# A graph network's first stage: the table of the nodes left out, edge lists turned on TensorE, and gathers that wait for TensorE's tiles

## The chip, the cores and the metric

One core of one Trainium2 chip runs the kernel. The metric is the device time of one execution in microseconds; the times given are medians of several runs. TensorE (PE in the profile) multiplies and transposes, VectorE (DVE) and ScalarE (ACT) do the arithmetic on tiles, GpSimd (POOL) issues the indirect gathers and scatters, SyncE (SP) issues the plain DMAs.

## What is computed

Four graph layers over 10,000 nodes of 768 values and 12,500 edges (2,500 drawn edges and one loop at each node), each followed by a residual and a layer norm. Only the first of them touches the change:

```python
def gat_conv(x, src, dst, W, a_src, a_dst, bias, H, C, n):
    h = (x @ W).reshape(n, H, C)
    s_src = (h * a_src).sum(-1)
    s_dst = (h * a_dst).sum(-1)
    e = leaky_relu(s_src[src] + s_dst[dst], 0.2)
    emax = segment_max(e, dst, num_segments=n)
    ee = exp(e - emax[dst])
    denom = segment_sum(ee, dst, num_segments=n)
    alpha = ee / denom[dst]
    out = segment_sum(alpha[:, :, None] * h[src], dst, num_segments=n)
    return out.reshape(n, H * C) + bias

# first layer
out1 = gat_conv(x_norm, src, dst, W1, a_src1, a_dst1, b1, 4, 192, N)
out2 = gat_conv(out1, src, dst, W2, a_src2, a_dst2, b2, 2, 96, N)
return concatenate([x, out2], axis=-1) @ Wu + bu

# later layers, per edge
norm = dinv[src] * dinv[dst]      # dinv = 1 / sqrt(degree)
```

## The kernel before

All of the change lies in the first stage, `first_layers`. It sends 2 x 79 tiles of 128 nodes through TensorE. Tiles 0 to 78 are the normalised x times the folded weights `w1` (792 columns: h1 and the scores of both attentions, worked into the weights); tiles 79 to 157 are x times `wu`. A tile is six transposes (`turn_over`, L1123) and 36 matmuls with split operands (`multiply`, L1139). DVE takes the statistics, makes the low part (`low`, L666) and empties the product (`end`, L674 to L679); ACT normalises and makes the high part; SP loads x four tiles ahead and stores the results four tiles behind (`load`, `store`).

Beside the tiles runs the graph work. Each engine's program is written as a row of such pieces, and `bg.to(t)` runs the engine's own tile steps up to step t before the next piece. So a piece has a fixed place between two tiles on each engine, and a wait in it holds up the engine's tiles behind it. The constants `AT_...` set these places. In order:

- POOL places the edges that aren't loops as records (source, destination) in DRAM, `packed`: 25 turns of four indirect scatters (`place`, L458 to L463).
- PE counts the nodes' degrees with one-hot matmuls (L1154). DVE makes from them the number of own loops and 1/sqrt(degree) of each node; SP writes both as the table `nodes`, 79 x 128 rows of two floats (`AT_NODE`, L412).
- SP reads the records back: column-wise, one edge a partition and chunk of 128 (`sd_c`, L415), and row-wise, one chunk a partition (`sd_r`, L416), with each chunk's neighbours. DVE makes the index lists `src_i`, `dst_i` from `sd_c` and the marks of equal destinations from `sd_r`, in blocks at steps 30 to 34 (`AT_LISTS`, L724 to L770).
- POOL gathers `nodes` at both ends of the edges: 20 chunks, each of two indirect gathers of 128 rows (L479 to L484). DVE takes from it `edge_dinv` and `own_e` at step 68 (`AT_OWN`).
- First attention: POOL waits for all stores of tiles 0 to 78, clears its buffers, gathers the scores `sc1` (two gathers a chunk, 40 in all, L512 to L514), and DVE, PE and ACT weigh them at steps 90 to 97 (`AT_A`). Then come 20 chunks, one a tile: POOL gathers the rows of h1 into a ring of four, DVE folds them, PE adds them up, ACT copies, POOL puts them into `h2` (`put`, L542).
- Second attention: POOL clears `kept_rows`, gathers the rows of `h2` (40 gathers again, L580 to L582), and from step 127 (`AT_B`) they are weighed and, two chunks a tile, added up and put into `out2`.

With 2,500 edges drawn, 20 chunks hold all of them; the loops for more chunks (`rest_groups`) don't run. The stage ends when all engines are through; the next one then starts with a clearing on POOL.

## Time and profile before

| | us |
|---|---|
| median of 3 runs | 4335.33 (4334.88 to 4337.32) |
| profiled execution | 4339.43 |
| its span | 4337.6 |
| PE busy | 3720.0 (86%) |
| DVE busy | 2597.3 (60%) |
| ACT busy | 1178.5 (27%) |
| POOL busy | 625.8 (14%) |
| first stage, to PE's last matmul | about 1445 |

The busy time is a mean over stages with different limits. The windows view gives it by stretches; the granted clock (PEclk) is TensorE's, 1.00 being 2.4 GHz. In a timeline each row is one instruction or a few alike, with the idle time of its engine ahead of it and what ended it. "issue" stands for idle time in which the engine waited for nothing that the profile shows. Tile numbers in the text count the groups of six transposes of L1123 from 0.

### The profile page before, as it was taken

To read this page: it belongs to the slowest core of one execution; us is meant where nothing else is said; L and a number is where in the kernel's file an instruction comes from. 1 tells how busy PE (TensorE), PEld (TensorE's weight loads), DVE (VectorE), ACT (ScalarE), POOL (GpSimd) and SP (SyncE) were. 2 spreads that over 40 slices of the span, in tenths; PEclk is the share of its full clock that TensorE was granted. 3 is DMA by queue.
4 is the path that set the end of the run, shared out by engine and by line. 5 is a ranking of instruction groups with operands and counts; after the bars stand their busy time and mean duration, and the time that the engine had idled before them with its cause. 6 is when DMAs were issued, how large, how long until landed. Compare 5 with 4: busy or idle time off the path is not lost. (4 is left out here: it accounts for less than half of the span.)

```text
span 4337.6 us, 64010 instructions
## 1 busy us (share of the span) xinstructions
PE 3720.0 (86%) x21454; PEld 3436.2 (79%) x21454; DVE 2597.3 (60%) x4977; ACT 1178.5 (27%) x1691; POOL 625.8 (14%) x640
## 2 busy tenths in 40 slices
PE   6886999699799888026888699999699999699999
PEld 5886999599699544015888399999399999499999
DVE  4765886067142488275999377777244443377777
ACT  2221232122122344003555222222222222222222
POOL 5523000414400000512000400000400000400000
PEclk8987999799899999568999899999899999899999
DMA  4783566346333588116776544444644443666665
GB/s 102 127 189 111 181 192 191 95 133 206 112 104 112 159 250 247 24 55 186 246 251 237 207 155 166 173 172 145 223 161 173 170 167 128 210 220 231 225 225 184
DMA packets 370508, 742.21 MB, mean 171 GB/s; under 512 B 109269, under 2 KB 162215, under 8 KB 370368
## 3 DMA queue, kind: packets, MB, share of 16 engines
q1 hardware_dynamic: 275600, 503.06, 38.1%
q10 hardware_dynamic: 67584, 154.63, 9.1%
q0 software_dynamic: 27184, 82.71, 6.2%
q8 instruction: 82, 1.34, 0.1%
q14 instruction: 58, 0.48, 0.0%
HBM read 444.99 MB, written 301.21 MB: 172 GB/s over the span
## 5 line engine op out<-in xcount | busy, mean ns | idle before, releaser
L666 DVE TENSOR_TENSOR fr_lo<-fr_turned_ps,fr_hi 128x768 fp32r<-128x768 f32 x158 | 150.4, 952 | 339.4 <-ACT fr_hi L1009 331.4
L1139 PE MATMUL fr_prod<-fr_wu_hi,fr_hi 128*128 128x396 f32 x948 | 261.5, 356 | 19.4 <-issue 19.4
L1139 PE MATMUL fr_prod<-fr_wu_lo,fr_hi 128*128 128x396 f32 x948 | 254.2, 348 | 18.3 <-issue 18.3
L1139 PE MATMUL fr_prod<-fr_wu_hi,fr_lo 128*128 128x396 f32 x948 | 252.7, 346 | 18.6 <-issue 18.5
L1139 PE MATMUL fr_prod<-fr_w_hi,fr_hi 128*128 128x396 f32 x948 | 259.2, 354 | 8.8 <-issue 8.8
L1139 PE MATMUL fr_prod<-fr_w_lo,fr_hi 128*128 128x396 f32 x948 | 251.6, 346 | 13.8 <-issue 13.8
L1139 PE MATMUL fr_prod<-fr_w_hi,fr_lo 128*128 128x396 f32 x948 | 250.5, 345 | 11.3 <-issue 11.3
L1009 ACT ACTIVATE fr_hi<-fr_turned_ps 128x768 fp32r<-128x768 f32 x158 | 127.4, 806 | 472.1 <-PE fr_turned_ps L1123 309.6
L2116 DVE SCALAR_TENSOR_TENSOR c3a_y<-c3a_prod,dinv,next_const 128x768 f32<-128x768 f32 x79 | 80.4, 1018 | 289.3 <-PE c3a_prod L2270 289.3
L2270 PE MATMUL c3a_prod<-next_w_hi,c3a_hi 128*128 128x384 f32 x948 | 248.1, 342 | 0.0
L2270 PE MATMUL c3b_prod<-next_w_hi,c3b_hi 128*128 128x384 f32 x948 | 248.0, 342 | 0.0
L2270 PE MATMUL cv_prod<-next_w_hi,cv_hi 128*128 128x384 f32 x948 | 248.0, 342 | 0.0
L2270 PE MATMUL c3a_prod<-next_w_hi,c3a_lo 128*128 128x384 f32 x948 | 242.4, 336 | 0.0
L2270 PE MATMUL cv_prod<-next_w_hi,cv_lo 128*128 128x384 f32 x948 | 242.2, 336 | 0.0
L2270 PE MATMUL c3b_prod<-next_w_hi,c3b_lo 128*128 128x384 f32 x948 | 242.1, 336 | 0.0
L2270 PE MATMUL c3a_prod<-next_w_lo,c3a_hi 128*128 128x384 f32 x948 | 241.3, 335 | 0.0
L2270 PE MATMUL c3b_prod<-next_w_lo,c3b_hi 128*128 128x384 f32 x948 | 241.3, 335 | 0.0
L2270 PE MATMUL cv_prod<-next_w_lo,cv_hi 128*128 128x384 f32 x948 | 241.3, 335 | 0.0
L1412 PE MATMUL up_prod<-w_up,up_ot 128*128 128x396 f32 x632 | 225.3, 500 | 1.4 <-DVE up_y L1316 1.3
L1139 PEld LDWEIGHTS fr_prod<-fr_wu_lo,fr_hi 128*128 128x128 f32 x948 | 178.4, 191 | 23.3 <-issue 23.2
L1139 PEld LDWEIGHTS fr_prod<-fr_wu_hi,fr_lo 128*128 128x128 f32 x948 | 178.3, 191 | 22.3 <-issue 22.3
L1139 PEld LDWEIGHTS fr_prod<-fr_wu_hi,fr_hi 128*128 128x128 f32 x948 | 172.2, 191 | 22.9 <-issue 22.9
(480 smaller groups left out, 8585.4 us busy)
## 6 DMA issues: line engine op xcount, KB each, us to landing
fr_ins<-in_x_dram SPq DMA_DIRECT2D x156, 384.0 KB
h<-fr_outs SPq DMA_DIRECT2D x78, 396.0 KB
u<-fr_outs SPq DMA_DIRECT2D x78, 396.0 KB
up_ut<-u SPq DMA_DIRECT2D x78, 396.0 KB
agg<-fr_zrow SPq DMA_DIRECT2D x78, 390.0 KB
hds_agg<-agg SPq DMA_DIRECT2D x78, 390.0 KB
x<-up_x_o ACTq DMA_DIRECT2D x78, 384.0 KB
hds_row<-x SPq DMA_DIRECT2D x78, 384.0 KB
```

The source lines that it names most:

```text
L666: v.tensor_tensor(lo[:, s2, :, :], turned_ps[:, 0:KC, :], hi[:, s2, :, :].bitcast(F32), ALU.subtract).then_inc(split_done, 1)
L1009: nc.scalar.activation(hi[:, t % 2, :, :], turned_ps[:, 0:KC, :], ACT.Copy).then_inc(hi_done, 1)
L1139: made = nc.tensor.matmul(prods[s2][:, bank, 0:c1 - c0], l[:, s2, s, :], w[:, s, c0:c1], start=(s == 0 and i == 0), stop=(s == KC - 1 and ...
L1412: made = nc.tensor.matmul(prods[s2][:, half, 0:HALFC], ot[:, s2, k, :], g["w_up"][:, k, half * HALFC:(half + 1) * HALFC], start=(k == 0), ...
L2116: ec.link(dve, v.scalar_tensor_tensor(y3, p3, g["dinv"][:, bass.ds(t, 1)], c3, ALU.mult, ALU.add))
L2270: last = nc.tensor.matmul(prods[s2][:, bank, 0:c1 - c0], l[:, s2, s, :], w[:, s, c0:c1], start=(s == 0 and i == 0), stop=(s == S - 1 and i ...
```

## The change

- The table `nodes`, its write and its 40 gathers go. The rows of `sc1` get ten values in place of eight: the scores, and then the node's own loops and 1/sqrt(degree), so the gathers of the scores bring them too. DVE takes `edge_dinv` and `own_e` from these at `AT_A`; the transpose of `own_e` moves into the first hop of the first attention.
- The scores are kept for all tiles (`sc_o[:, t, :]`) and stored by a step of their own: tiles 18 to 78 with the tile, tiles 0 to 17 during steps 61 to 78.
- The column-wise reload `sd_c` goes. PE turns `sd_r` at step 30, DVE waits for it (`lists_up`).
- Each pair of score gathers on POOL waits until TensorE has turned 84 + 2c // 3 tiles, each pair of h2 gathers until it has turned 128 + c // 2.
- `AT_A` moves from 90 to 98, `AT_B` from 127 to 138.

```diff
-AT_A, AT_B = 90, 127
+AT_A, AT_B = 98, 138
...
-    nodes = dram("nodes", (NT * P, 2))
-    sc1 = dram("sc1", (N, 8))
+    sc1 = dram("sc1", (N, 10))
...
-        h2_o, sc_o = sb("h2_o", [P, UNROLL, HX]), sb("sc_o", [P, UNROLL, 4, 2])
+        h2_o, sc_o = sb("h2_o", [P, UNROLL, HX]), sb("sc_o", [P, NT, 10])
...
-                    sp.dma_start(tile_rows(sc1, t), sc_o[0:n, slot, :, :].rearrange("p h k -> p (h k)")).then_inc(stored[slot], 16)
...
+                if AT_NODE + 7 <= t < NT + 4:
+                    store_scores(t - 4)
+                if NT - AT_NODE - 3 <= t < NT:
+                    store_scores(t - (NT - AT_NODE - 3))
+
+            def store_scores(t):
+                sp.wait_ge(out_ready, 2 * t + 2)
+                sp.wait_ge(node_done, 1)
+                sp.dma_start(tile_rows(sc1, t), sc_o[0:rows_of(t), t, :]).then_inc(sc_stored, 16)
...
-            bg.to(AT_NODE + 2)
-            sp.wait_ge(node_done, 1)
-            sp.dma_start(nodes.rearrange("(t p) k -> p t k", p=P), pt["node"][:, :, :]).then_inc(node_out, 16)
             bg.to(AT_RELOAD)
             sp.wait_ge(packs, 16 * EC)
-            sp.dma_start(pt["sd_c"][:, :, :], packed[P:P + NC * P, :].rearrange("(c p) w -> p c w", p=P)).then_inc(reloaded, 16)
             sp.dma_start(pt["sd_r"][:, :, :], packed[P:P + NC * P, :].rearrange("(c j) w -> c j w", j=P)).then_inc(reloaded, 16)
...
-            for c in range(SC):
-                rows_from(nodes, pt["nd_src"][:, c, :], g["src_i"][:, c:c + 1], nd_in)
-                rows_from(nodes, pt["nd_dst"][:, c, :], g["dst_i"][:, c:c + 1], nd_in)
...
+            pool.wait_ge(sc_stored, 16 * NT)
...
             for c in range(SC):
+                pool.wait_ge(turned, NT + 5 + 2 * c // 3)
                 rows_from(sc1, gt["from_src"][:, c, :], g["src_i"][:, c:c + 1], la.scores_in)
                 rows_from(sc1, gt["from_dst"][:, c, :], g["dst_i"][:, c:c + 1], la.scores_in)
...
             for c in range(SC):
+                pool.wait_ge(turned, AT_B - 10 + c // 2)
                 rows_from(h2, kept_rows[:, c, 0, :], g["src_i"][:, c:c + 1], lb.scores_in)
                 rows_from(h2, kept_rows[:, c, 1, :], g["dst_i"][:, c:c + 1], lb.scores_in)
...
             bg.to(AT_LISTS)
-            dve.wait_ge(reloaded, 64)
+            dve.wait_ge(reloaded, 48)
+            dve.wait_ge(lists_up, 1)
...
-            link(v.tensor_copy(g["src_i"][:, 0:NC], sd_c[:, :, 0]))
-            v.tensor_copy(g["dst_i"][:, 0:NC], sd_c[:, :, 1]).then_inc(lists_done, 1)
+            link(v.tensor_copy(g["src_i"][:, 0:NC], pb[:, 0:NC]))
+            link(v.tensor_copy(pt["dst_c"][:, :], pb[:, 128:128 + NC]))
+            v.tensor_copy(g["dst_i"][:, 0:NC], pt["dst_c"][:, :]).then_inc(lists_done, 1)
...
             bg.to(AT_OWN)
-            dve.wait_ge(nd_fetched, 1)
-            link(v.tensor_copy(g["edge_dinv"][:, :], pt["nd_src"][:, :, 1]))
-            v.tensor_copy(own_e[:, :], pt["nd_dst"][:, :, 0]).then_inc(own_up, 1)
...
             bg.to(AT_A)
             fs, fd = gt["from_src"], gt["from_dst"]
+            dve.wait_ge(la.fetched, 1)
+            link(v.tensor_copy(g["edge_dinv"][:, :], fs[:, :, 9]))
+            link(v.tensor_copy(own_e[:, :], fd[:, :, 8]))
...
+            bg.to(AT_LISTS)
+            pe.wait_ge(reloaded, 48)
+            nc.tensor.transpose(pb[:, 0:NC], pt["sd_r"][:, :, 0], idn)
+            nc.tensor.transpose(pb[:, 128:128 + NC], pt["sd_r"][:, :, 1], idn).then_inc(lists_up, 1)
```

POOL, at the start of the first attention's score gathers (`fr_from_src` and `fr_from_dst` are the scores at the edges' sources and destinations, `sc` is the table in DRAM). Before:

```order
120 L506 MEMSET fr_from_src 128x800 [waits fr_stored3,fr_stored2,fr_own_done,fr_stored1,fr_stored0]
121 L507 MEMSET fr_from_dst 128x800
122 L508 MEMSET fr_rows 128x6336
123 L471 DMA fr_from_src<-sc,src_i 128x8 [waits fr_a_zeroed]
124 L471 DMA fr_from_dst<-sc,dst_i 128x8
125 L471 DMA fr_from_src<-sc,src_i 128x8
126 L471 DMA fr_from_dst<-sc,dst_i 128x8
127 L471 DMA fr_from_src<-sc,src_i 128x8
```
and now:

```order
36 L482 MEMSET fr_from_src 128x1000 [waits fr_stored3,fr_sc_stored,fr_stored2,fr_own_done,fr_stored1,fr_stored0]
37 L483 MEMSET fr_from_dst 128x1000
38 L484 MEMSET fr_rows 128x6336
39 L473 DMA fr_from_src<-sc,src_i 128x10 [waits fr_turned,fr_a_zeroed]
40 L473 DMA fr_from_dst<-sc,dst_i 128x10
41 L473 DMA fr_from_src<-sc,src_i 128x10 [waits fr_turned]
42 L473 DMA fr_from_dst<-sc,dst_i 128x10
43 L473 DMA fr_from_src<-sc,src_i 128x10 [waits fr_turned]
```
The clearing waits for one semaphore more, and each pair of gathers waits for `turned`, TensorE's count of turned tiles.

SP's queue, after the stores of tile 12 and at the reload of the lists (`fr_node` is the table of the nodes, `fr_sd_c` and `fr_sd_r` the two forms of the list, `fr_ins` the next tile of x). Before:

```order
95 L382 DMA out<-fr_h_o 128x192
96 L412 DMA nodes<-fr_node 128x79x2 [waits fr_node_done]
97 L373 DMA fr_ins<-in_x_dram 128x768 [waits fr_built]
98 L392 DMA agg<-fr_zrow 256x1x390
```
```order
150 L382 DMA out<-fr_h_o 128x192
151 L415 DMA fr_sd_c<-packed 128x100x2 [waits fr_packs]
152 L416 DMA fr_sd_r<-packed 100x256
153 L417 DMA fr_prv<-packed 100x1
154 L419 DMA fr_nxt<-packed 100x1
155 L373 DMA fr_ins<-in_x_dram 128x768 [waits fr_built]
```
and now, at the reload:

```order
129 L378 DMA h<-fr_h_o 128x196
130 L379 DMA out<-fr_h_o 128x192
131 L401 DMA sc<-fr_sc_o 128x10 [waits fr_node_done,fr_out_ready]
132 L418 DMA fr_sd_r<-packed 100x256 [waits fr_packs]
133 L419 DMA fr_prv<-packed 100x1
134 L421 DMA fr_nxt<-packed 100x1
135 L371 DMA fr_ins<-in_x_dram 128x768 [waits fr_built]
```
The write of the table is gone, the reload is one DMA shorter, and the scores' store, now 10 values wide, stands behind the stores of the tile.

PE, between the matmuls of tile 28 and the transposes of tile 30 (`fr_pb` is a PSUM bank, `fr_turned_ps` the transposed tile). Before:

```order
662 L1139 MATMUL fr_prod<-fr_w_hi,fr_lo 128x396 x2
663 L1123 MATMUL fr_turned_ps<-ident,fr_xn 128x128 [waits fr_split_done,fr_built]
664 L1123 MATMUL fr_turned_ps<-ident,fr_xn 128x128 x5
665 L1139 MATMUL fr_prod<-fr_w_hi,fr_hi 128x396 [waits fr_prod_read,fr_split_done]
666 L1139 MATMUL fr_prod<-fr_w_hi,fr_hi 128x396
```
and now:

```order
662 L1117 MATMUL fr_prod<-fr_w_hi,fr_lo 128x396 x2
663 L1140 MATMUL fr_pb<-ident,fr_sd_r 128x100 [waits fr_reloaded]
664 L1141 MATMUL fr_pb<-ident,fr_sd_r 128x100
665 L1101 MATMUL fr_turned_ps<-ident,fr_xn 128x128 [waits fr_split_done,fr_built]
666 L1101 MATMUL fr_turned_ps<-ident,fr_xn 128x128 x5
667 L1117 MATMUL fr_prod<-fr_w_hi,fr_hi 128x396 [waits fr_prod_read,fr_split_done]
```
Two transposes of the lists stand ahead of the tile, with a wait for the reload.

## Rows read from the trace of the kernel before

**Rows 1.** Windows: us; busy (count) of PE, PEld, DVE, ACT, POOL; PEclk; DMA share; GB/s.
```profile
245.60:331.60 86.00, 86.00 (x506) 85.42 (x504) 60.73 (x109) 23.98 (x34) 22.49 (x29) 1.00 0.77 199
...
956.20:1081.90 125.70, 125.70 (x739) 125.25 (x738) 100.03 (x81) 29.87 (x48) 59.08 (x46) 1.00 0.64 209
```

**Rows 2.** Timeline, PE: start, us, instruction, [idle before <-releaser]; first transposes of nine tiles.
```profile
197.99 0.60 PE L1123 MATMUL fr_turned_ps<-ident,fr_xn 128*128 128x128 f32 x4
...
236.42 0.87 PE L1123 MATMUL fr_turned_ps<-ident,fr_xn 128*128 128x128 f32 x3 [31.13 <-DVE fr_lo L666]
...
245.64 0.82 PE L1123 MATMUL fr_turned_ps<-ident,fr_xn 128*128 128x128 f32 x6
...
331.64 0.82 PE L1123 MATMUL fr_turned_ps<-ident,fr_xn 128*128 128x128 f32 x6
...
405.51 0.71 PE L1123 MATMUL fr_turned_ps<-ident,fr_xn 128*128 128x128 f32 x5
...
768.80 0.82 PE L1123 MATMUL fr_turned_ps<-ident,fr_ins 128*128 128x128 f32 x6
...
832.55 0.82 PE L1123 MATMUL fr_turned_ps<-ident,fr_ins 128*128 128x128 f32 x6
...
1118.48 0.71 PE L1123 MATMUL fr_turned_ps<-ident,fr_ins 128*128 128x128 f32 x5
...
1171.61 0.82 PE L1123 MATMUL fr_turned_ps<-ident,fr_ins 128*128 128x128 f32 x6
```

**Rows 3.** Timeline, SP's queue: the nodes table, and two DMAs behind small-packet ones.
```profile
196.77 0.38 SPq L412 DMA_DIRECT2D nodes<-fr_node  x1
197.19 23.78 SPq L373 DMA_DIRECT2D fr_ins<-in_x_dram  x1
...
286.71 6.60 SPq L416 DMA_DIRECT2D fr_sd_r<-packed  x1
```

**Rows 4.** Timeline, PE: matmuls with idle time ahead of them.
```profile
340.64 0.34 PE L1139 MATMUL fr_prod<-fr_w_lo,fr_hi 128*128 128x396 f32 x1 [0.67 <-issue]
...
386.45 0.49 PE L1139 MATMUL fr_prod<-fr_w_lo,fr_hi 128*128 128x396 f32 x1 [1.80 <-issue]
...
1120.06 0.27 PE L1123 MATMUL fr_turned_ps<-ident,fr_ins 128*128 128x128 f32 x1 [0.87 <-issue]
```

**Rows 5.** Timeline, POOL: first and last of 40 gathers, in two bursts.
```profile
329.76 1.06 POOL L471 DMA_INDIRECT fr_nd_src<-nodes,src_i  x1 [48.91 <-DVE dst_i L728]
...
380.55 0.99 POOL L471 DMA_INDIRECT fr_nd_dst<-nodes,dst_i  x1 [0.31 <-issue]
...
1103.71 1.05 POOL L471 DMA_INDIRECT fr_rows<-h,src_i  x1 [0.81 <-POOL fr_stage L578]
...
1154.59 1.00 POOL L471 DMA_INDIRECT fr_rows<-h,dst_i  x1 [0.31 <-issue]
```

**Rows 6.** Timeline, POOL: turns of the placing loop, and one put of the first attention.
```profile
177.88 0.33 POOL L458 COPY fr_ix<-fr_rank_i 125x4 int32 x1 [2.01 <-DMA packed<-fr_rec,fr_ix]
...
221.98 1.20 POOL L463 DMA_INDIRECT packed<-fr_rec,fr_ix  x1 [22.66 <-issue]
...
234.37 0.19 POOL L458 COPY fr_ix<-fr_rank_i 125x4 int32 x1 [9.69 <-DMA packed<-fr_rec,fr_ix]
...
957.56 1.04 POOL L542 DMA_INDIRECT h<-fr_sums,put_i  x1 [3.44 <-ACT fr_sums L1046]
```

**Rows 7.** Timeline, DVE's blocks for the lists, and PE's start of tile 35.
```profile
328.15 0.06 DVE L725 MEMSET src_i<- 128x4 int32 x1
...
332.54 0.23 DVE L735 COPY same_b<-same_f 100x127 f32<-100x127 f32 x1
...
338.18 1.59 DVE L737 COPY same_f<-same_f 100x1408 f32<-100x1408 f32 x1
...
405.71 0.25 DVE L760 COPY row_f<-fr_pb 12x100 f32<-12x100 f32 x1 [3.07 <-PE fr_pb L1166]
...
414.24 0.84 PE L1123 MATMUL fr_turned_ps<-ident,fr_xn 128*128 128x128 f32 x6 [1.42 <-DVE fr_lo L666]
```
## What I expect of the change

> **What bounds the kernel now.** I read the busy time by stretches first. In the first stage, where 158 tiles pass TensorE, an undisturbed stretch shows PE busy for all of its 86 us at full granted clock (1.00) [rows 1]: TensorE is the bound, and a tile costs the 86.00 us between the starts of tiles 18 and 30 over 12, 7.17 us [rows 2]. Then I read PE's timeline for the starts of tiles, to find what is not 7.17 us. Four places stand out [rows 2]:
> - tiles 16 and 17 take 245.64 - 197.99 = 47.65 us;
> - tiles 30 to 33 take 405.51 - 331.64 = 73.87 us;
> - tiles 83 and 84 take 832.55 - 768.80 = 63.75 us;
> - tiles 122 and 123 take 1171.61 - 1118.48 = 53.13 us.
>
> The first is a wait: PE stands still for 31.13 us for DVE's split, at tile 17 [rows 2]. SP's queue names its cause: the nodes table is issued at 196.77, and the load of x behind it takes 23.78 us to issue, where the load after the packed lists takes 6.60 [rows 3]. The table is 79 x 128 rows of 8 bytes; the load behind it comes too late for DVE.
> The other three are not waits for a semaphore: PE's idle time is put down to "issue", and it comes in gaps of 0.7 to 1.8 us between single matmuls [rows 4]. They coincide with POOL's three bursts of 40 indirect gathers, 1.3 us apart without a pause (329.76 to 380.55; 1103.71 to 1154.59) [rows 5]. PE isn't hit at once: 340.64 - 329.76 = 10.9 us pass in the one, 1120.06 - 1103.71 = 16.4 in the other, so some 8 to 12 gathers are free. I read this as a reserve ahead of PE that a long burst empties and a pause fills up again.
>
> **The change, part by part.**
> 1. The nodes table is not written. SP's issue, its 10,112 small packets and the late load go. What is late next at that place? POOL's loop that places the records: the same packets held it too (a stop of 22.66 us within a turn, and 9.69 where 2.01 is usual at its end, [rows 6]), so it moves up by about 30 us together with SP, which waits for its end at tile 26. SP could wait 0 to 5 us there; the reload that it issues now delays the next load by 6.60 us [rows 3] and PE's tiles 18 to 29 stay at 7.17, so that much cover exists, and the 6.60 itself goes with the column-wise reload. Taken: 47.65 - 2 x 7.17 = 33.3 us gained.
> 2. The burst of 40 gathers from the table goes altogether, and with it the slow time in tiles 30 to 33. But the lists now come by two transposes on TensorE, and DVE has to wait for them. DVE comes to its block at 328.15, 3.5 us ahead of PE's tile 30 (331.64); a like exchange stands at 405.71: DVE starts its copies 0.20 us after the tile's start at 405.51, having waited 3.07 us, eleven small operations of some 0.27 us follow, and PE's next tile begins at 414.24, 5.6 us after them, with an idle 1.42 [rows 2, 7]. The new block: 332.77 - 328.15 = 4.6 us and one copy of 0.2. Tile 30 becomes 0.2 + 4.8 + 5.6 = 10.6 us. Tile 31 has the two copies of 1.6 us [rows 7]: 3.2 + 5.5 = 8.7. Tile 32 has eleven small operations, by the same 0.25 some 2.7: 2.7 + 5.5 = 8.2. Tile 33 has nine small matmuls for the rows, now as before: 7.17 + 0.9 = 8.1. The transposes themselves: 0.3. Sum 35.9 in place of 73.87: 38.0 gained. This stall of about 6 us was hidden by the burst and now shows; if DVE catches up better, the gain is at most 6 us larger.
> 3. The gathers of the scores (first attention) wait for TensorE's tiles, two pairs and one pair in turn, from tile 83 to 95. The waits stand on POOL alone; behind them on POOL are only the next gathers, the first six gathers of h rows and the puts. DVE comes for the scores at tile 98 (it was 90). The last gathers are let go when tile 95 is turned; four take 5.2 us and about 2 to land and tell, DVE asks after 14 us. Cover 7 us: cost nothing. If all slow time goes: 63.75 - 14.34 = 49.4 us gained.
> 4. The same for the gathers of h2 rows (second attention), two pairs a tile from tile 127 to 136, DVE at 138: 53.13 - 14.34 = 38.8 us gained. Here POOL starts late: its clearing ends at tile 128, so twelve gathers run as one train of 15.6 us before the waits space them. DVE asks about 9 us after the last pairs are let go and they need 7: cover 2 us.
> 5. The attentions end later (138 + 18 = tile 156 of 158). Their last two puts leave with over one tile, 7 us, and the stage's last stores to go: nothing. Their work on DVE and PE is the same, moved. The store of scores goes from one place of SP's queue to another, two a step in 18 steps; SP has gaps. Two copies and an addition of 0.25 us on DVE, one transpose on PE: under 1 us.
>
> **What spacing leaves.** The trace has gathers and scatters in small groups already, and they bound the cost. POOL's placing loop issues four scatters, 1.2 us each and 0.3 apart, and then pauses some 3 us, 2.01 of them for the landing [rows 6], 25 times; PE shows no such gap beside it. The first attention's row gathers come three a tile (2 gathers, one put, then 3.44 idle [rows 6]); over 125.70 us PE is busy 125.70 with 739 matmuls [rows 1], 46 a tile, so 16 tiles of 7.86, which is 7.17 and the four matmuls of the sums. So groups of up to four with a pause cost 0. The other end: each gather costs what it costs in a burst, 49.4 + 38.8 = 88.2 us for both, as now. I take a value near the first end, since both rows there are the same work at nearly the same spacing: 5 us, for the two trains that remain longer (about ten gathers at the end of the first attention's, twelve at the start of the second's, as against 8 to 12 free).
>
> The Trainium skill, "Runtime: NRT & Kernel Launch", section "Instruction fetch mechanics", speaks against my reading: TensorE holds 2048 instructions, is refilled in blocks of 256, and the fetch is mostly hidden. By that a reserve would not run dry in 11 to 16 us, the gaps would be a price of each gather, and spacing would give nothing (rival A). The trace does not agree with the plain form of it, since gathers at three a tile show no gap at all.
>
> **Rivals.**
> A. Spacing gives nothing: the price is per gather, whenever it runs. Then parts 1 and 2 alone stand: 4335.3 - 33.3 - 38.0 = 4264 us. Against it: the free first 10.9 and 16.4 us, and the rows of small groups. For it: neither is a group of four gathers in every tile of 7.17.
> B. The reserve fills too slowly at four a tile. A group of four is 5.2 us, the pause 2. In the second attention up to 1 to 2 us could be lost a tile over ten tiles, in the first half of that: 15 to 30 us more, 4195 to 4211 us.
> C. Slower than before: each group hits PE at once and PE needs about 5 us after its end to come back (after 380.55 + 1.0 it still had a gap before 386.45 [rows 4, 5]). Seven groups of four (5.2 + 5), six of two (2.6 + 5), ten of four: 219 us slow, of which 88% lost is 193, against 88 that go. 4335.3 - 71.3 + 105 = 4369 us. It decides if a pause of less than 5 us is no pause. Against it: the placing loop pauses for 3 and PE shows nothing.
> D. The list exchange goes worse: PE's transposes wait for the reload. It lands long before (issued 30 us earlier). Worth under 10 us.
>
> **The numbers.** 33.3 + 38.0 + 49.4 + 38.8 = 159.5, less 5 = 154.5 us. The profiled execution took 4339.4 us (span 4337.6); the median of the runs is 4335.3, 0.1% below, and I take the sum off that: 4181 us. Chances: the forecast 0.80, B 0.10, A 0.05, C 0.03, something else 0.02. The range: below, all of the 5 and the 6 us of part 2 come back, 4170, with a few us for what one execution can't show, 4166; above it takes in B: 4215. About 0.2%, 9 us, is what a measurement of this kernel can tell from no change: faster by more 0.96, within 0.01, slower 0.03.
>
> **What would show it.** Right: PE's tiles 16 and 17 at 7.17; tile 30 near 10.6 with an idle time that DVE's split ends; no "issue" gaps over 0.7 us on PE in the first stage, or a few at tiles 97 and 129; granted clock 1.00 from 200 us on; later stages unchanged. Wrong: "issue" gaps on PE within groups of four (B) or throughout the tiles with gathers (A, C); DVE waiting for the scores at tile 98 or 138; SP waiting for the placing loop until PE stands.

## The result, and the profile after

The changed kernel takes 4183.3 us (median of 4 runs, 4179.4 to 4185.8) beside 4336.3 us (4334.9 to 4338.4, 4 runs) of the kernel before on the same chip: a ratio of 0.9646, 95% interval 0.9629 to 0.9663. The forecast was 4181 us in a range of 4166 to 4215. The profiled execution took 4185.8 us, its span 4184.0.

The gain is all in the first stage: its last tile starts at 1272.4 us where it was 1430.8, 158.4 earlier. What follows that start takes 2911.7 us (before 2906.9), 4.8 more. No part of that rest is changed, and it lies between 2902.7 and 2911.7 in the other executions below, so I read no effect into it.

By places (between starts of tiles on TensorE, us):

| Tiles | before | after | gained | forecast |
|---|---|---|---|---|
| 16, 17 (nodes table) | 47.65 | 14.36 | 33.3 | 33.3 |
| 18 to 29 | 86.0 | 88.0 | -2.0 | 0 |
| 30 to 33 (lists) | 73.87 | 35.67 | 38.2 | 38.0 |
| 83, 84 (gathers of scores) | 63.75 | 14.32 | 49.4 | 49.4 |
| 122, 123 (gathers of h2 rows) | 53.13 | 15.63 | 37.5 | 38.8 |
| all other tiles together | | | 2.0 | -5 |

The windows of the changed kernel (columns as in [rows 1]) cover the table's place, the lists' block, and the two stretches from the first spaced gather to the last:
```profile
198.34:212.70 14.36, 14.36 (x85) 14.28 (x84) 10.37 (x21) 5.50 (x8) 4.17 (x7) 1.00 0.67 209
300.69:336.36 35.67, 30.31 (x178) 28.96 (x177) 29.99 (x62) 8.10 (x12) 0.00 (x0) 1.00 0.48 154
701.76:792.45 90.69, 90.69 (x532) 90.23 (x532) 12.43 (x13) 19.10 (x25) 40.00 (x40) 1.00 0.39 118
1041.59:1106.47 64.88, 64.75 (x380) 64.23 (x379) 8.63 (x9) 13.82 (x18) 40.05 (x40) 1.00 0.53 171
```
In the last two PE is busy for all of the time but 0.13 us, at granted clock 1.00. The windows of the kernel before over the first two bursts read quite otherwise:
```profile
331.64:405.51 73.87, 39.89 (x177) 33.49 (x176) 27.17 (x56) 8.19 (x12) 38.42 (x40) 0.68 0.27 76
768.80:832.55 63.75, 25.09 (x85) 18.93 (x84) 1.92 (x2) 3.06 (x4) 39.62 (x41) 0.60 0.26 72
```
In the second window, 85 matmuls had 25.09 us of busy time in 63.75, at a mean granted clock of 0.60 (the levels are 1.2 and 2.4 GHz, 0.5 and 1). So a burst costs in two ways: idle gaps, and matmuls that take more busy time, since they no longer overlap and the clock is lower.

PE's timeline after, first transposes of tiles 16, 18 and 26, the second of the two new transposes, and tiles 30, 31, 32 and 34 (for [rows 2] and [rows 4]):
```profile
198.34 0.82 PE L1101 MATMUL fr_turned_ps<-ident,fr_xn 128*128 128x128 f32 x6
...
212.70 0.82 PE L1101 MATMUL fr_turned_ps<-ident,fr_xn 128*128 128x128 f32 x6
...
271.74 0.85 PE L1101 MATMUL fr_turned_ps<-ident,fr_xn 128*128 128x128 f32 x6 [1.43 <-DVE fr_lo L644]
...
300.57 0.28 PE L1141 MATMUL fr_pb<-ident,fr_sd_r 100*128 100x100 f32 x1
300.69 0.82 PE L1101 MATMUL fr_turned_ps<-ident,fr_xn 128*128 128x128 f32 x6
...
311.47 0.85 PE L1101 MATMUL fr_turned_ps<-ident,fr_xn 128*128 128x128 f32 x6 [3.43 <-DVE fr_lo L644]
...
320.09 0.84 PE L1101 MATMUL fr_turned_ps<-ident,fr_xn 128*128 128x128 f32 x6 [1.25 <-DVE fr_lo L644]
...
336.36 0.82 PE L1101 MATMUL fr_turned_ps<-ident,fr_xn 128*128 128x128 f32 x6
```
The stall of 31.13 us is gone. Tile 30 shows the exchange with DVE that had been hidden under the burst: PE waits 3.43 us for the split, then 1.25 at tile 32. Between 80 us and the end of the first stage the kernel before has 74 idle times of over 0.2 us on PE that end with "issue", 101.1 us in sum; the changed one has none of that length.

DVE's lists block after (for [rows 7]), its start, its last small operation, and the split for tile 30:
```profile
300.99 0.06 DVE L704 MEMSET src_i<- 128x4 int32 x1 [3.93 <-PE fr_pb L1141]
...
305.71 0.23 DVE L715 COPY same_b<-same_f 100x127 f32<-100x127 f32 x1
...
310.37 0.96 DVE L644 TENSOR_TENSOR fr_lo<-fr_turned_ps,fr_hi 128x768 fp32r<-128x768 f32 x1
```
SP's queue after (for [rows 3]), around the reload of the lists; no idle time is given for it, so the starts tell it:
```profile
252.92 0.40 SPq L401 DMA_DIRECT2D sc<-fr_sc_o  x1
261.77 0.30 SPq L418 DMA_DIRECT2D fr_sd_r<-packed  x1
```
And POOL's, the last scatter of the placing loop (for [rows 6]), the spaced gathers of the first attention and the first train of the second (for [rows 5]):
```profile
259.30 1.19 POOL L465 DMA_INDIRECT packed<-fr_rec,fr_ix  x1 [0.30 <-issue]
...
708.79 1.00 POOL L473 DMA_INDIRECT fr_from_src<-sc,src_i  x1 [2.04 <-PE fr_turned_ps L1101]
...
715.95 1.00 POOL L473 DMA_INDIRECT fr_from_src<-sc,src_i  x1 [4.87 <-PE fr_turned_ps L1101]
...
1041.59 1.05 POOL L473 DMA_INDIRECT fr_rows<-h,src_i  x1 [0.80 <-POOL fr_stage L555]
...
1056.18 1.00 POOL L473 DMA_INDIRECT fr_rows<-h,dst_i  x1 [0.30 <-issue]
1059.63 1.00 POOL L473 DMA_INDIRECT fr_rows<-h,src_i  x1 [2.45 <-PE fr_turned_ps L1101]
```
POOL's list of waits adds them up: in the first attention 13 waits for TensorE's tiles, 50.9 us in all. Tiles 83 to 97 take 107.4 us beside them, 7.16 each, so PE loses nothing by them.

### The profile page after: what moved, and what is told of

The parts are those of the page before. It is cut to its first block and busy times, and to the rows that moved or that the text cites. A ratio compares the mean times of both kernels' runs of the same rounds, so it can differ in the third digit from the quotient of the medians.

```text
span 4184.0 us, 64009 instructions
## 1 busy us (share of the span) xinstructions
PE 3690.6 (88%) x21456; PEld 3423.5 (82%) x21456; DVE 2600.0 (62%) x4978; ACT 1181.5 (28%) x1691; POOL 584.2 (14%) x597
## 5 line engine op out<-in xcount | busy, mean ns | idle before, releaser
L2158 ACT ACTIVATE c3a_hi<-c3a_turned_ps 128x768 fp32r<-128x768 f32 x79 | 64.3, 814 | 435.7 <-PE c3a_turned_ps L2233 435.7
L2244 PE MATMUL hds_prod<-hds_w_st,hds_hi 128*128 128x128 f32 x948 | 184.0, 276 | 0.0
L2245 PE MATMUL hds_prod<-hds_w_st,hds_hi 128*128 128x128 f32 x948 | 183.8, 276 | 0.0
```

The source lines that it names most:

```text
L2158: nc.scalar.activation(hi[:, s2, :, :], turned_ps[:, 0:S, :], ACT.Copy).then_inc(hi_done, 1)
L2244: nc.tensor.matmul(o, hi[:, s2, s, :], w_st[:, 0, :], start=True, stop=False)
L2245: last = nc.tensor.matmul(o, hi[:, s2, KC + s, :], w_st[:, 1, :], start=False, stop=True)
```

## The experiments

One thing has to be known for all that follows. The kernel before ran beside every group of experiments, and it took one of two times: 4203.8 to 4204.8 us (medians of two groups, 13 and 15 runs) or 4331.8 to 4340.7 us (three groups, 7 to 9 runs each, and the result above). Within a group it never changed, and one chip showed both at different times. I call them groups L (low, about 4204) and H (high, about 4335); all that is said of a train of gathers depends on which it was.

The theory: a long train of indirect gathers on POOL starves TensorE; the waits for tiles keep the groups short enough. The first rival is A of the forecast, that spacing gives nothing.

### Groups L: the parts alone

**no_waits**: the changed kernel without its two waits.
```diff
-                pool.wait_ge(turned, NT + 5 + 2 * c // 3)
...
-                pool.wait_ge(turned, AT_B - 10 + c // 2)
```


> The changed kernel without the two waits for TensorE's turned tiles; all else as changed, the places of the attentions too. Theory (a long train of gathers empties a reserve ahead of TensorE): the two slow stretches come back, each beginning 11 to 16 us after its first gather, 49.4 + 38.8 = 88 us more than the changed kernel, 4271 us. Rival (the waits do nothing, the gain of these two stretches came from the moved places or from the traffic of the table): 4183 us, no issue gaps.

Measured: 4177.8 us (4175.3 to 4181.6), ratio 0.9940 [0.9925, 0.9955] to a kernel before of 4204.8. The windows over both trains:
```profile
695.00:800.00 105.00, 105.00 (x619) 104.44 (x618) 13.65 (x15) 22.58 (x30) 42.41 (x44) 1.00 0.45 141
1040.00:1115.00 75.00, 75.00 (x439) 74.60 (x439) 12.65 (x17) 16.36 (x22) 38.41 (x40) 1.00 0.54 164
```
Trains of 40 gathers, and PE is busy throughout (the trains begin at 690.39 and 1037.94 us, and no idle time on PE from 80 us to the end of the stage is an "issue" of over 0.2 us). In this group a train costs nothing, and my theory seemed to fall.

**spaced_only**: the kernel before with the waits and the two later places (AT_A 98, AT_B 138).
```diff
-AT_A, AT_B = 90, 127
+AT_A, AT_B = 98, 138
...
+                pool.wait_ge(turned, NT + 5 + 2 * c // 3)
...
+                pool.wait_ge(turned, AT_B - 10 + c // 2)
```


> The kernel before with only the waits for TensorE's tiles ahead of the score and h2 gathers and the places of the attentions moved (98 and 138); the table, its gathers and the column-wise reload stay. The last runs showed the kernel before at 4204.8 us where it took 4336.3 beside the changed one, and a burst of 40 gathers without slow TensorE: so there are two conditions of the chip or its loading. Theory (the slow stretches are TensorE's behind a train of gathers, in one condition alone): where the kernel before takes about 4336, this one takes 88 less, 4248 us; where it takes about 4205, this one takes the same within 5 us, as there is nothing to take away. Rival (the condition changed with something in the kernel or its load order): this one differs from the kernel before by neither 88 nor 0.

Measured: 4202.7 us, ratio 0.9999 [0.9989, 1.0008]. The burst of 40 table gathers is still in it, and its window shows PE busy for 47.35 of 50.82 us at granted clock 1.00, where the same burst gave 39.89 of 73.87 at 0.68 in the first trace:
```profile
324.48:375.30 50.82, 47.35 (x280) 45.92 (x279) 43.75 (x92) 13.27 (x20) 38.94 (x40) 1.00 0.57 170
```
Its tiles 30 to 33 take 31.85 us. That accounts for nearly all of the difference between the two times of the kernel before: without the costs of the bursts its first trace would be shorter by 73.87 - 31.85 = 42.0, 49.4 and 38.8, in sum 130.2 us; the medians differ by 4336.3 - 4204.8 = 131.5. One more place differs in these two traces: tiles 16 and 17, with the stall of the table, take 41.29 us here and 47.65 there. What the waits are worth to the kernel before in a group H was not run; no_waits_again tests them there in the changed one.

**table_written**: the changed kernel, but SP writes the nodes table as before (nothing reads it).
```diff
+            sp.dma_start(g["nodes"].rearrange("(t p) k -> p t k", p=P), sc_o[:, :, 8:10]).then_inc(node_out, 16)
```


> The changed kernel with the table of the nodes written again from the score tile at the old place in SP's queue (79 x 128 pieces of 8 bytes), and not read. Theory: the load behind it comes late, TensorE stands for about 31 us at tile 17, 33 us more: 4216 us. Rival (most of that stall was the table together with something else that is gone now, such as the reload or the old score stores): under 10 us more, 4193 us at most.

Measured: 4208.3 us (10 runs), ratio 1.0010 [1.0001, 1.0019]; 30.5 us above no_waits of the same group. SP's queue and PE:
```profile
198.10 0.38 SPq L421 DMA_DIRECT2D nodes<-fr_sc_o  x1
198.52 20.34 SPq L374 DMA_DIRECT2D fr_ins<-in_x_dram  x1
...
232.60 1.51 PE L1108 MATMUL fr_turned_ps<-ident,fr_xn 128*128 128x128 f32 x6 [25.75 <-DVE fr_lo L651]
```
The load behind the table takes 20.34 us to issue and PE stands for 25.75, as in [rows 2, 3] (there 23.78 and 31.13). This part needs no train of gathers: it is worth 27.6 us here by the tiles (41.92 less 14.36) and 33.3 in the first pair of traces. Whether the 5.7 us between them belong to the condition H was not tested.

**lists_reloaded**: the lists come by the column-wise load again, without the transposes.
```diff
+            sp.dma_start(pt["sd_c"][:, :, :], packed[P:P + NC * P, :].rearrange("(c p) w -> p c w", p=P)).then_inc(reloaded, 16)
...
-            nc.tensor.transpose(pb[:, 0:NC], pt["sd_r"][:, :, 0], idn)
-            nc.tensor.transpose(pb[:, 128:128 + NC], pt["sd_r"][:, :, 1], idn).then_inc(lists_up, 1)
```


> The changed kernel with the lists reloaded column-wise from DRAM as before, and without the two transposes. Theory: DVE no longer waits for TensorE at tile 30 (3.5 us and the 0.3 of the transposes come back), but SP has by now waited 8 us for the placing loop, so the 6.6 us of the small packets add to the late load at tile 25 instead of being covered: about 4 us less and 7 us more, 4186 us. Rival (the reload is still covered): 4179 us, so that the transposes only cost.

Measured: 4185.4 us, ratio 0.9952 [0.9939, 0.9966], 7.5 us above no_waits. SP's queue, and PE's tile 26:
```profile
261.56 6.38 SPq L419 DMA_DIRECT2D fr_sd_r<-packed  x1
...
277.98 1.51 PE L1100 MATMUL fr_turned_ps<-ident,fr_xn 128*128 128x128 f32 x6 [8.26 <-DVE fr_lo L645]
```
The load costs 6.38 us of SP's queue at the moment at which SP is already late from its wait for the placing loop, and PE stands 8.26 us: tiles 18 to 29 take 96.4 us. In return tiles 30 to 33 take 31.7, 4.0 less than with the transposes. These are the two terms that I had expected, about 7 more and 4 less. That the time came out at 4186 is partly luck: I had reckoned from 4183, and no_waits stands at 4177.8 in this group. By the traces the stage is 3.5 us longer at these tiles; the medians say 7.5, with runs between 4176 and 4188.

**turned_earlier**: the two transposes one step earlier.
```diff
-            bg.to(AT_LISTS)
+            bg.to(AT_LISTS - 1)
             pe.wait_ge(reloaded, 48)
```


> The changed kernel with the two transposes one tile earlier on TensorE (ahead of tile 29 in place of tile 30). Theory: DVE finds the lists turned when it comes to its block, its wait of about 4 us ahead of tile 30 goes, tile 30 takes 7.3 us in place of 10.8, tile 31 some 0.4 less: 4 us less, 4179 us. Rival (DVE's block of 4.8 us is itself what is late): under 1 us less.

Measured: 4174.2 us, ratio 0.9930 [0.9916, 0.9943]; tiles 30 to 33 take 31.84 us, tile 30 7.18:
```profile
299.81 0.82 PE L1101 MATMUL fr_turned_ps<-ident,fr_xn 128*128 128x128 f32 x6
```
Beside no_waits of the same group (35.73) that is 3.9 us less. So some 3.8 us of the lists' cost is DVE waiting for PE to come to the transposes.

### Groups H: what a train does to TensorE

**changed_again** is the changed kernel once more, so that it stands beside the next.

> The changed kernel itself, beside the kernel before on whichever chip this is. Theory (two conditions; in one, trains of gathers slow TensorE, in the other not): where the kernel before takes about 4205, the changed one gains the stall of the table alone, 27 us: 4177 us; where it takes about 4336, it gains 153: 4183 us. Rival (the changed kernel keeps its gain everywhere): 4205 - 153 = 4052 us, which nothing in its trace leaves room for.

Measured: 4181.8 us, ratio 0.9651 [0.9637, 0.9665]; tiles 83 to 97 take 107.4 us, no idle time on PE of over 0.2 us that ends with "issue".

**no_waits_again** is no_waits, unaltered.

> The changed kernel without the two waits for TensorE's tiles, once more, beside the changed one on one chip. Theory: where the kernel before takes about 4205, the waits are worth nothing, the same as the changed kernel within 3 us; where it takes about 4336, 88 us more than the changed kernel. Rival (the waits cost something of their own, by holding POOL): this one is faster by more than 3 us where trains don't slow TensorE.

Measured: 4266.0 us (4261.2 to 4270.9), ratio 0.9845 [0.9832, 0.9859]; 84 us above changed_again. The same program lost nothing in the group L. POOL's first gather of each train, and PE's first gap in each:
```profile
694.86 1.06 POOL L473 DMA_INDIRECT fr_from_src<-sc,src_i  x1 [0.84 <-POOL fr_rows L484]
...
1092.50 1.05 POOL L473 DMA_INDIRECT fr_rows<-h,src_i  x1 [0.80 <-POOL fr_stage L554]
...
708.55 0.44 PE L1115 MATMUL fr_prod<-fr_wu_hi,fr_lo 128*128 128x396 f32 x1 [0.23 <-issue]
...
1109.53 0.34 PE L1115 MATMUL fr_prod<-fr_wu_hi,fr_hi 128*128 128x396 f32 x1 [0.93 <-issue]
```
Three windows of the first: up to the first gap, to the end of the train, and behind it.
```profile
695.00:708.30 13.30, 13.30 (x79) 12.92 (x77) 0.96 (x1) 1.54 (x2) 10.25 (x11) 1.00 0.36 98
708.30:747.00 38.70, 10.06 (x24) 5.47 (x24) 0.96 (x1) 1.53 (x2) 29.66 (x30) 0.56 0.14 27
747.00:765.00 18.00, 8.90 (x27) 7.23 (x27) 0.96 (x1) 1.53 (x2) 6.09 (x7) 0.53 0.55 180
```
The first matmul behind a gap comes 13.7 and 17.0 us after the train's first gather; up to there the train is free. Then PE is busy for 10.06 of 38.70 us with 24 matmuls: 0.42 us of busy time each in place of 13.30 / 79 = 0.17, at a granted clock of 0.56. Not all of that is the clock. In the busy stretch a single matmul of the product takes 0.34 to 0.35 us too, but it overlaps its neighbours; in the slowed one it takes 0.44 to 0.46 and stands alone (means of the lines view). Up to 765 us that is 37.7 us of idle time and 10.4 more of busy time; the last of it falls beside the six gathers of h1 rows that follow the train from 748.71 on; tiles 83 to 97 lose 156.1 - 107.4 = 48.7. Rival A is refuted here: the price is not per gather.

**longer_groups**: groups of 8 gathers every three tiles in the first attention, of 16, 16 and 8 every four tiles in the second.
```diff
-                pool.wait_ge(turned, NT + 5 + 2 * c // 3)
+                pool.wait_ge(turned, NT + 5 + 3 * (c // 4))
...
-                pool.wait_ge(turned, AT_B - 10 + c // 2)
+                pool.wait_ge(turned, AT_B - 10 + 4 * (c // 8))
```


> The changed kernel with longer groups between the waits: score gathers in groups of 8 (10.4 us) every three tiles, h2 gathers in groups of 16, 16 and 8 (20.8 us) every four. Theory (a reserve of 11 to 17 us is used up by a train and filled again in the pause): where trains slow TensorE (the kernel before at about 4335), the groups of 8 cost nothing, save the last with the six h1 gathers behind it (a few us), the groups of 16 run dry after some 16 us and cost 5 to 10 us each: 10 to 25 us more than the changed kernel, 4192 to 4207 us. Rival (what counts is the mean rate of gathers, the same here): as the changed kernel, 4182 us. Where trains don't slow it, 4178 us by both.

Measured: 4201.1 us, ratio 0.9682 [0.9667, 0.9696]. Groups of 8 cost nothing (tiles 83 to 97: 107.4). Each group of 16 costs one tile 8.1 us (tiles 130 and 133: 15.31 and 15.20 for 7.18). The last gather of the first such group, which began at 1042.89, the first of the second, and PE's first gap in each:
```profile
1062.51 1.00 POOL L473 DMA_INDIRECT fr_rows<-h,dst_i  x1 [0.30 <-issue]
1075.03 1.00 POOL L473 DMA_INDIRECT fr_rows<-h,src_i  x1 [11.52 <-PE fr_turned_ps L1101]
...
1058.68 0.32 PE L1101 MATMUL fr_turned_ps<-ident,fr_ins 128*128 128x128 f32 x1 [0.28 <-issue]
...
1090.81 0.52 PE L1117 MATMUL fr_prod<-fr_wu_hi,fr_lo 128*128 128x396 f32 x2 [1.31 <-issue]
```
In both, the first matmul behind a gap starts 15.8 us into the group. The mean rate of gathers is that of the changed kernel, four a tile, so the rival that only the mean rate counts is refuted: what is issued within some 16 us counts. The second group began 11.5 us after the end of the first and had the full free time again, so a pause of 11.5 us is enough to restore it.

**short_and_plain**: no waits; the first attention gathers 32 rows in place of 128 with each instruction, the second moves plain blocks of rows. It leaves out most of the gathering, so its output is another.
```diff
+                rows_from(sc1, gt["from_src"][0:32, c, :], g["src_i"][0:32, c:c + 1], la.scores_in)
+                rows_from(sc1, gt["from_dst"][0:32, c, :], g["dst_i"][0:32, c:c + 1], la.scores_in)
...
+                pool.dma_start(kept_rows[:, c, 0, :], h2[c * P:(c + 1) * P, :]).then_inc(lb.scores_in, 16)
+                pool.dma_start(kept_rows[:, c, 1, :], h2[(c + 20) * P:(c + 21) * P, :]).then_inc(lb.scores_in, 16)
```


> No waits for TensorE's tiles. The score gathers bring 32 rows each in place of 128, and the 40 gathers of h2 rows are 40 plain DMAs of as many bytes from POOL's queue (rows 0 to 5119 in place of the edges'; the scores of most edges and the rows of all are left out so). Theory 1 (the train of transfers and their descriptors slows TensorE): where trains do slow it, the first train slows it less than the 49 us of 128 rows, and the second by what it did. Theory 2 (the indirect instruction on POOL itself does it): the first slows it as before, the second not at all. Sum where trains slow it: theory 1 4183 + 0 to 20 + 38, theory 2 4183 + 49 us; else 4178 us.

Measured: 4232.0 us, ratio 0.9756 [0.9741, 0.9771]. The first attention's train slows PE as much with a quarter of the rows (tiles 83 to 97 take 157.55 us, 50.2 more; from 12.9 us on). Its first gather and PE's first gap:
```profile
692.00 0.98 POOL L473 DMA_INDIRECT fr_from_src<-sc,src_i  x1 [0.86 <-POOL fr_rows L484]
...
704.85 0.51 PE L1115 MATMUL fr_prod<-fr_wu_hi,fr_lo 128*128 128x396 f32 x2 [0.59 <-issue]
```
The windows over the slowed part of that train and over the whole of the plain one, which slows nothing:
```profile
704.80:740.57 35.77, 7.29 (x17) 3.86 (x16) 0.96 (x1) 1.53 (x2) 26.93 (x30) 0.55 0.10 25
1090.81:1112.05 21.24, 21.24 (x126) 21.12 (x125) 2.87 (x3) 4.61 (x6) 21.24 (x40) 1.00 0.85 263
```
So the number of rows does not matter, and a plain transfer from the same engine is free. The plain train was only 21.2 us long, though, which left a doubt.

**spread_by_pool** takes up that doubt and asks whether a pause is needed at all. Without the waits for tiles, POOL clears a piece of a buffer after each score gather, and the gathers of h2 rows become 80 plain transfers of half the width; these leave the gathering out, so the output is another.
```diff
-                pool.wait_ge(turned, NT + 5 + 2 * c // 3)
                 rows_from(sc1, gt["from_src"][:, c, :], g["src_i"][:, c:c + 1], la.scores_in)
+                nc.gpsimd.memset(stage[:, 0:2, :, :], 0.0).then_inc(paused, 1)
+                pool.wait_ge(paused, 2 * c + 1)
                 rows_from(sc1, gt["from_dst"][:, c, :], g["dst_i"][:, c:c + 1], la.scores_in)
+                nc.gpsimd.memset(stage[:, 0:2, :, :], 0.0).then_inc(paused, 1)
+                pool.wait_ge(paused, 2 * c + 2)
...
-                pool.wait_ge(turned, AT_B - 10 + c // 2)
...
+                for k in range(2):
+                    for i in range(2):
+                        pool.dma_start(kept_rows[:, c, k, 98 * i:98 * i + 98], h2[(c + 20 * k) * P:(c + 20 * k + 1) * P, 98 * i:98 * i + 98]).then_inc(lb.scores_in, 16)
```


> The changed kernel without its two waits for tiles, and with both bursts of first attention A and B altered. A: the 40 score gathers stay, but after each one GpSimd clears a piece of a buffer that nothing uses then (2 x 2 x 196 numbers a lane, an estimate of 0.7 to 0.8 us), so a gather is issued every 2.0 to 2.1 us in place of 1.30, in one go of some 82 us. That is the mean rate of the changed kernel (3 to 4 a tile of 7.16 us: 1.8 to 2.4 us each) without its free stretches of 2 to 3 us between groups. B: 80 plain transfers of 128 rows x 98 numbers from GpSimd's queue in place of 40 gathers, so that the train of plain transfers lasts about 42 us, as long as the gathers' train, and not 21 us as in short_and_plain; this part leaves the gathering out, so the output of that layer is another. Theory 1 (what starves TensorE is the mean rate of indirect gathers, and plain transfers don't do it however long): neither burst costs anything, 4178 to 4186 us. Rival 1 (a train needs a real pause, its length decides): the gathers of A slow TensorE from 13 to 17 us after the start of the train, by up to 50 us: 4200 to 4235. Rival 2 (a train of any transfers from GpSimd's queue starves TensorE once it is long enough): issue gaps at B from 13 to 17 us in, 15 to 35 us more, 4195 to 4220. All of it holds if this is a session where the kernel before takes about 4335 us; where it takes about 4204 us no train costs anything and the run tells nothing of this: 4175 to 4185.

Measured: 4180.3 us (4176.6 to 4182.4), ratio 0.9647 [0.9631, 0.9663]. POOL's timeline at the start of the one train, and the merged row of the other:
```profile
693.61 1.06 POOL L474 DMA_INDIRECT fr_from_src<-sc,src_i  x1 [0.84 <-POOL fr_rows L485]
694.68 0.77 POOL L489 MEMSET fr_stage<- 128x784 f32 x1
696.24 1.01 POOL L474 DMA_INDIRECT fr_from_dst<-sc,dst_i  x1 [0.79 <-POOL fr_stage L489]
...
1043.68 42.17 POOL L564 DMA_DIRECT2D fr_rows<-h  x80 [0.30 <-POOL fr_stage L559]
```
The windows over the two:
```profile
693.61:797.50 103.89, 103.89 (x613) 103.33 (x612) 14.36 (x15) 23.02 (x30) 71.68 (x82) 1.00 0.37 116
1043.68:1085.85 42.17, 42.17 (x249) 41.92 (x248) 5.74 (x6) 9.22 (x12) 42.17 (x80) 1.00 0.69 196
```
PE is busy throughout both. A plain train of 42.17 us, over twice as long as the free time of a train of gathers, costs nothing; in the profile's list of DMA queues its packets stand under the same queue as those of the gathers (q0, software_dynamic), so it is the indirect instruction on POOL that tells the two apart. And 40 gathers cost nothing in one train of some 100 us if each follows the last by 2.55 us (longer than the 2.0 to 2.1 that I had set out to get, since the chain of the clearing and its wait adds 0.8) in place of 1.30. No pause of several us is needed: the 1.5 us between the end of one gather and the start of the next are enough. Between 1.30 and 2.55 us a steady rate was not tried.

**later_reload**: both small losses of the changed kernel taken back, SP's reload a step later, the lists' block too, the transposes a step ahead of it.
```diff
-AT_HIST, AT_NODE, AT_RELOAD, AT_LISTS = 4, 15, 26, 30
+AT_HIST, AT_NODE, AT_RELOAD, AT_LISTS = 4, 15, 27, 31
...
-            bg.to(AT_LISTS)
+            bg.to(AT_LISTS - 1)
             pe.wait_ge(reloaded, 48)
```


> The changed kernel with the reload of the lists one tile later on SP (27) and the blocks of the lists one tile later (31), and the transposes one tile ahead of DVE's first block, as in the run with turned_earlier. Theory: SP waits 1 us for the placing loop in place of 8, tile 25 takes 7.2 in place of 8.8 to 9.6, and DVE's wait of about 4 us at the lists goes: 5 to 6 us less than the changed kernel, 4177 where trains slow TensorE and 4172 where not. Rival (one tile later DVE's blocks meet other work): no gain over the changed kernel.

Measured: 4178.0 us (4175.2 to 4183.3), ratio 0.9632 [0.9618, 0.9645]. Tiles 18 to 29 take 86.4 us, 30 to 33 30.8, and the last tile of the stage starts 7.8 us earlier than in the changed kernel; 3.2 of these stand ahead of the stage's first tile, which the edit doesn't touch, so 4.6 are left. The ratios' intervals overlap (0.9651 [0.9637, 0.9665] for the changed kernel), so these 4 to 5 us rest on the traces.

## Why the prediction was right, point by point

**1, the table.** Right: 33.3 us forecast and measured, by the mechanism named; table_written brings the stall back. The step on what is late next failed in size. SP was to wait 0 to 5 us for the placing loop, under cover. It waited 8.4: from 252.92 + 0.40 to 261.77, just behind the loop's last scatter (259.30 + 1.19). The loop ended only 19.9 us earlier than before (259.30 in place of 279.17), where SP came 33.3 earlier. I had moved the loop by the two stops of [rows 6], some 30 us; but by POOL's timeline the stretch from the turn in which the table was written to the last turn became only 26.2 us shorter (195.58 to 273.64; 201.87 to 253.76), and that turn itself began 6.3 us later in this execution. The load behind was late for DVE, PE stood for 1.43 us, and tiles 18 to 29 lost 2.0. The cover of 6.60 us that I leant on was overrun by 8.4 - 6.6 = 1.8 us, about what was lost; and lists_reloaded shows what would have come with the column-wise load still in the queue: 10 us.

**2, the lists.** Right within 0.2 us: 10.78, 8.62, 8.06 and 8.22 us for tiles 30 to 33, forecast 10.6, 8.7, 8.2 and 8.1. DVE waited 3.93 us for the transposes (3.5 forecast) and took 4.95 from there to its last small copy (4.8). The gain of 38.2 holds in groups H alone; in groups L this part costs 3.8 us (35.7 in place of 31.85). No run puts the table's 40 gathers back by themselves in a group H; that they cost 42 us there rests on the first trace beside spaced_only, and on what trains of the same kind do in no_waits_again.

**3 and 4, the spaced gathers.** Right in place and price: 49.4 and 37.5 of 49.4 and 38.8. The 1.3 us that the second is short of are no train's: tiles 122 and 123 now carry sums of the moved first attention, 7.81 us a tile. The cause that I gave, the indirect gathers in a train, stands: no_waits_again loses 84 us. I had read the gaps as 0.7 to 1.8 us; in the bursts of the kernel before they are 0.2 to 2.4 us long, and 3.7 once. A reserve that is emptied at a gather every 1.30 us, is not at one every 2.55, and is full again after 11.5 us without one fits all of these runs (free time 10.9 to 17.1 us over all traces). But it is a picture: what holds the reserve stays open. Nothing of this was to be seen in the profile of before: that these 88 us, and the 42 of the first burst, are there in some groups of runs and not in others. My chances had no case for it: that the changed kernel was first timed in a group H, as the profile of before had been, is luck. In a group L the time would have come out near 4181 too, but beside a kernel before of 4204.8, so that the gain forecast, 154.5 us, would have been wrong. In groups L no_waits, which there equals the changed kernel in all but its waits, stands 26.9 us below the kernel before. By tiles, beside spaced_only, 26.9 come at the table (41.29 less 14.36), 2.8 go at tiles 18 to 29 and 3.9 at the lists, which leaves 20.2; the rest is 2.8 us ahead of the first tile and small differences at others. The changed kernel itself was not run in such a group.

**The 5 us for what trains remain.** Too careful: they cost 0.3 to 0.4 us. The first attention's last four gathers are followed by a pause before the row gathers, and no gap shows there. The twelve of the second's start last 15.6 us (1041.59 to 1057.18), at the very edge of the free time, and that edge shows: 17.1 us after their first gather, at 1058.65, PE has one "issue" gap of 0.13 us, and tile 130 takes 7.45 us (7.57 in changed_again, with the same gap), where it takes 7.18 in no_waits, a run of a group L.

**Rivals.** A is refuted in groups H; in groups L spacing does give nothing, but because a train costs nothing there, not because each gather costs. B and C: no gap within groups of four, and the granted clock stays at 1.00 through both stretches. D: tile 30 as forecast.

The queues of instructions bear on what a train takes from PE. In the profile's list of DMA queues (packets, MB, share of 16 engines) q8 is the one that I take for PE's, by its pace. It moved one block (0.02 MB) from 695 to 765 us in no_waits_again, beside 79 + 24 + 27 = 130 matmuls:
```profile
q8 instruction: 1, 0.02, 0.1%
```
and three in no_waits, beside some 410 matmuls (by 619 in 105 us):
```profile
q8 instruction: 3, 0.05, 0.3%
```
So in both the blocks follow the matmuls, one for 130 to 140 of them, and no block is missing in the slowed run. Its one block set out between 713.5 and 714.0 us:
```profile
q8 instruction: 1, 0.02, 19.9%
```
The gaps had begun 5 us before, and they went on to 760 us: from 714 to 765 PE ran 45 matmuls, a third of what goes with a block. So, if q8 is PE's, TensorE had these gaps with a block just landed, and a late block is not their cause. What PE lacks there stays open. The Trainium skill, "Runtime: NRT & Kernel Launch", section "Instruction fetch mechanics", says that crossing a block's boundary is mostly hidden. These rows don't speak against it; but what the forecast drew from it, that spacing would then give nothing, fell in groups H.

## What to carry to other kernels

When TensorE's idle time ends with "issue" in many small gaps, look at what GpSimd issues at that time: here, in groups H, a run of indirect gathers at 1.3 us each starves it after 11 to 17 us, and spreading them (groups of up to 8, or 2.55 us each) costs nothing if nobody waits for the rows. The write of the table, 10,112 pieces of 8 bytes, holds its queue for 20 to 24 us, and whatever is issued behind it is late; the column-wise load of the lists holds it for 6.4. To turn the lists on TensorE for 0.3 us is cheaper than that load, if it is done one step ahead of the reader (4174.2 beside 4185.4 us). And before a gain is booked, the kernel before should be timed at more than one occasion: most of this one exists on some of them alone.

## What the runs showed of the hardware that I had not expected

- **Two conditions.** The same program takes 4204 us on some occasions and 4332 to 4341 on others, fixed within a group of runs and seen on one and the same chip. Nearly all of the difference is what trains of indirect gathers cost TensorE. What sets it was not found.
- **The indirect instruction, not its rows.** A gather of 32 rows slows TensorE as one of 128 does, though POOL's row is 0.92 us and not 1.00; a plain transfer from the same queue, 0.53 us each, doesn't.
- **The gaps keep a step of their own.** In the slowed stretch of no_waits_again the matmuls behind gaps start 1.4, 2.1 or 2.8 us apart:
```profile
738.00 0.49 PE L1115 MATMUL fr_prod<-fr_wu_hi,fr_hi 128*128 128x396 f32 x1 [2.31 <-issue]
740.10 0.49 PE L1115 MATMUL fr_prod<-fr_wu_hi,fr_hi 128*128 128x396 f32 x1 [1.61 <-issue]
```
  The next are at 742.90 and 745.00. All are multiples of 0.7 us, where the gathers go out every 1.30. Why was not found.
- **The clock falls with the gaps.** The granted clock was 0.56 from 708.3 to 747 us and 0.53 behind it, having been 1.00 while PE was busy without gaps; PE was busy for a quarter of the first of these stretches. With waits of 3.43 and 1.25 us, in tiles 30 to 33 of the changed kernel, it stayed at 1.00.
